# Loading the x0 steps of a CIN tower straight from their rows in DRAM, without the four-fold copy

## What is computed

```python
def cin(embeddings, W0, W1, W2):
    x0 = xk = embeddings                       # (1024, 32, 16)
    outs = []
    for W in (W0, W1, W2):                     # W0 (32, 32, 64), W1 and W2 (32, 64, 64)
        xk = relu(einsum('bmd,bhd,mhk->bkd', x0, xk, W))
        outs.append(sum(xk, axis=2))
    return concatenate(outs, axis=1)           # (1024, 192)

e = stack([tbl_f[ids[:, f]] for f in range(32)], axis=1)
h = concatenate([cin(e, W0, W1, W2), dense_ctx], axis=1)
h = maximum(h @ W_top1 + b_top1, 0)
h = maximum(h @ W_top2 + b_top2, 0)
y = h @ W_top3
```

## Time and profile before

| | before |
|---|---|
| device time, median of 3 runs | 718.49 us |
| lowest and highest | 717.80 and 718.72 us |
| span of the profiled execution | 715.9 us |
| DVE busy | 600.3 us, 84% |
| PE busy | 599.1 us, 84% |
| POOL busy | 524.6 us, 73% |
| SP's DMA queue | 178.22 MB, 66.0% of 16 engines' time |
| `x0_copies` written from `x0_rows` | 28 DMAs, 12 MB |
| loads from `x0_copies` | 83 DMAs |

### The profile page before, as it was taken

How to read it: one execution, slowest core, us unless ns; L and a number is a source line. 1 busy time by engine, 2 the same in 40 slices (tenths; PEclk the granted TensorE clock), 3 DMA queues, 4 the chain that set the end, 5 groups by cost and what they waited for, 6 DMA issues and landing times.

```text
span 715.9 us, 8322 instructions
## 1 busy us (share of the span) xinstructions
PE 599.1 (84%) x2592; PEld 192.4 (27%) x2592; DVE 600.3 (84%) x442; ACT 237.5 (33%) x388; POOL 524.6 (73%) x383
## 2 busy tenths in 40 slices
PE   2057859898987998898698988897979999999998
PEld 1053213232322222222222222232322232223333
DVE  0004997899999999999969999999999999999750
ACT  1004251615233241616124251616152526151413
POOL 6777778778888888787587888688887385738530
PEclk9569988999999999999899999999999999999999
DMA  4239899596949877595919877596939696927000
GB/s 102 65 89 393 311 352 388 199 381 244 369 152 329 347 271 293 187 402 216 396 43 334 340 270 295 184 400 223 399 125 358 245 390 240 393 87 278 0 1 0
DMA packets 64662, 180.58 MB, mean 252 GB/s; under 512 B 10033, under 2 KB 22193, under 8 KB 64642
## 3 DMA queue, kind: packets, MB, share of 16 engines
q1 hardware_dynamic: 56450, 178.22, 66.0%
q0 software_dynamic: 8192, 2.11, 2.6%
HBM read 176.63 MB, written 16.26 MB: 269 GB/s over the span
## 4 chain that ended last, share of the span: by engine, by line
POOL 34%; issue 20%; PE 15%; DVE 15%; DMA 8%; ACT 6%; SPq 1%; DVEq 0%; POOLq 0%; ACTq 0%
POOL gathered L482 18%; POOL pool_ring L521 12%; PE acc L797 11%; DVE dve_ring L667 10%; DMA x_wide<-x_copies 8%; POOL pool_ring L482 4%; ACT x_ps L572 3%; ACT x_sb L582 2%; PE x_ps L823 2%; DVE z_half L682 2%; DVE l_tiles L704 2%; DVE features L689 1%; ACT layer_out L576 1%; SPq L358 0%; DMA idx<-in_ids 0%
## 5 line engine op out<-in xcount | busy, mean ns | idle before, releaser
L667 DVE TENSOR_TENSOR dve_ring<-x_wide,x_ps 128x1024 f32<-128x1024 f32 (+1 forms) x328 | 446.4, 1423 | 30.6 <-ACT x_ps L572 26.1
L797 PE MATMUL acc<-dve_ring,w_sb 128*64 128x512 f32 x1576 | 380.7, 607 | 40.4 <-DVE dve_ring L667 38.5
L521 POOL TENSOR_TENSOR pool_ring<-x_wide,x_sb 128x1024 f32<-128x1024 f32 x118 | 280.0, 2379 | 79.8 <-ACT x_sb L582 46.8
L482 POOL DMA_INDIRECT gathered<-in_tbl,idx x224 | 213.5, 953 | 72.9 <-issue 64.8
L797 PEld LDWEIGHTS acc<-dve_ring,w_sb 128*64 128x64 f32 x1576 | 106.3, 139 | 297.9 <-issue 147.3
L797 PE MATMUL acc<-pool_ring,w_sb 128*64 128x512 f32 x472 | 127.0, 618 | 29.1 <-POOL pool_ring L521 29.1
L572 ACT ACTIVATE x_ps<-acc 64x512 f32<-64x512 f32 x128 | 73.0, 570 | 134.3 <-PE acc L797 125.0
L576 ACT ACTIVATE layer_out<-acc 128x512 f32<-128x512 f32 x48 | 28.7, 597 | 165.0 <-PE acc L797 164.2
L582 ACT COPY x_sb<-layer_out 64x512 f32<-64x512 f32 x128 | 79.0, 617 | 3.4
L704 DVE TENSOR_TENSOR l_tiles<-x_wide,x_rot_ps 128x1024 f32<-128x1024 f32 x32 | 38.5, 1209 | 47.8 <-DMA x_wide<-x_copies 47.8
L769 PE MATMUL acc<-l_tiles,w_sb 128*64 128x512 f32 x256 | 61.2, 599 | 4.0 <-DVE l_tiles L704 3.5
(11 more groups left out here) (36 smaller groups left out, 100.4 us busy)
## 6 DMA issues: line engine op xcount, KB each, us to landing
x_wide<-x_copies SPq DMA_DIRECT2D x58, 2048.0 KB, 11.7
l_tiles<-x_copies SPq DMA_DIRECT2D x16, 1024.0 KB
x_copies<-x_rows SPq DMA_DIRECT2D x14, 768.0 KB
x_wide<-x_copies SPq DMA_DIRECT2D x6, 1536.0 KB, 13.4
x_rot<-x_rows SPq DMA_DIRECT2D x64, 128.0 KB, 4.2
gathered<-in_tbl,idx POOLq DMA_INDIRECT x224, 2.4
x_wide<-x_copies SPq DMA_DIRECT2D x3, 1024.0 KB, 9.0
x_rows<-x_t SPq DMA_DIRECT2D x7, 256.0 KB, 6.7
```

What stands on the lines that cost most here:

```text
L482: pool.indirect_dma_start(into[:, f * DIM:(f + 1) * DIM], None, tables[f], bass.IndirectOffsetOnAxis(ap=idx[:, slot, f:f + 1], axis=0)).th ...
L521: nc.gpsimd.tensor_tensor(pool_ring[:, slot, :], x0_step(h, layer, t), x_sb[layer - 1][:], ALU.mult).then_inc(pool_made, 1)
L667: nc.vector.tensor_tensor(dve_ring[:, slot:slot + width, :], x0_step(h, layer, t, width).rearrange("p (s n) -> p s n", n=WIDE), x_ps[layer ...
L797: last = nc.tensor.matmul(acc[h][c * HK:(c + 1) * HK, :], w_sb[layer - 1][:, step_at(layer, t), :], tile[:, c * CHUNK:(c + 1) * CHUNK], st ...
```

## The change

`x0_copies`, its writes and its two semaphores are gone. `load_steps` now takes its rows from `x0_rows`, and issues one DMA for each step of 128 partitions: 512 KB, whose source runs over 32 rows, each named four times by a dimension of stride 0, with 4 KB for each name. A block is four such DMAs, a load of layer 0's operands two, and the waits on their semaphores count accordingly. `load_operands` waits for the staging of the tile where it waited for the copies. At the start the parts are staged without a wait after each, and one wait stands before the loads.

```diff
-            def copy_rows(tile, h, first, last):
-                src = rows_of(tile)[first:last, h * WIDE:(h + 1) * WIDE].unsqueeze(1).broadcast_to([last - first, Q, WIDE])
-                dst = x0_copies[bass.ts(2 * tile + h, COPIED * Q), :].rearrange("(f q) n -> f q n", q=Q)
-                sp.dma_start(dst[first - FIRST_FIELD:last - FIRST_FIELD], src).then_inc(x0_copied[h], 16)
...
             def load_steps(dst, tile, h, first, apart, sem):
-                rows = x0_copies[bass.ts(2 * tile + h, COPIED * Q), :][first * Q:]
+                rows = rows_of(tile)[FIRST_FIELD + first:, h * WIDE:(h + 1) * WIDE]
                 row = rows.ap[0][0]
-                src = bass.AP(rows.tensor, rows.offset,
-                              [[row, P], [apart * Q * row, dst.ap[1][1]], list(rows.ap[1])])
-                sp.dma_start(dst, src).then_inc(sem, 16)
+                for i in range(dst.shape[1]):
+                    src = bass.AP(rows.tensor, rows.offset + i * apart * row, [[row, FIELDS], [0, Q], [1, WIDE]])
+                    sp.dma_start(dst[:, i, :], src).then_inc(sem, 16)
...
             def load_operands(tile, h, p):
-                sp.wait_ge(x0_copied[h], copied(tile))
+                sp.wait_ge(x0_staged, staged(tile))
...
                     stage(0, place, (j, j + 1))
                     parts += 1
-                sp.wait_ge(x0_staged, 16 * parts)
-                for h in range(2):
-                    for field, place in fields:
-                        copy_rows(0, h, max(field, FIRST_FIELD), min(field + F_TILE, FIRST_FIELD + COPIED))
+            sp.wait_ge(x0_staged, 16 * parts)
             load_rot(0, 0)
-            sp.wait_ge(x0_copied[0], copied(0))
             load_near(0, 0)
...
-                    if start:
-                        copy_tile(1, 1)
-                    if h == 1 and there(it, 2):
-                        copy_tile(it + 2, 0)
-                        copy_tile(it + 2, 1)
...
-                eng.wait_ge(near_loaded[p], 16)
+                eng.wait_ge(near_loaded[p], 32)
...
         def block_loads(it, h, block):
-            return 16 * (it + 1) if block < 2 else 16 * (2 * it + h + 1)
+            if block >= 2:
+                return 16 * BLOCK * (2 * it + h + 1)
+            if isinstance(it, int) and 2 * it + h < NEAR_FIRST:
+                return 16 * (BLOCK - 1)
+            return 16 * BLOCK * (it + 1) - (32 if h == 0 else 16)
...
-                        dve.wait_ge(far_loaded, 16 * (p + 1))
+                        dve.wait_ge(far_loaded, 32 * (p + 1))
```

More of the change, by code:

```diff
@@ L41 @@
 FIRST_FIELD = 4
-COPIED = FIELDS + STEPS
 ROW_TILES = ROWS // P
@@ L154, in cin_tower @@
         x0_rows = nc.dram_tensor("x0_rows", (TILES * KEPT, DIM * P), F32, kind="Internal").ap()
-        x0_copies = nc.dram_tensor("x0_copies", (TILES * 2 * COPIED * Q, WIDE), F32, kind="Internal").ap()
         x0_wide = sb("x0_wide", [P, 6, BLOCK * WIDE])
@@ L222, in cin_tower @@
         rot_loaded = sem("rot_loaded")
-        x0_copied = [sem(f"x0_copied{h}") for h in range(2)]
         near_loaded = [sem(f"near_loaded{p}") for p in range(NEAR_FIRST)]
@@ L274, in block_loads @@
         def block_loads(it, h, block):
-            return 16 * (it + 1) if block < 2 else 16 * (2 * it + h + 1)
+            if block >= 2:
[3 more added lines that the diff above has]
+            return 16 * BLOCK * (it + 1) - (32 if h == 0 else 16)
         def staged(tile):
             return 16 * (KEPT // F_TILE) + 32 * tile
-        def copied(tile):
-            return 16 * (KEPT // F_TILE + tile)
         def rows_of(tile):
@@ L334, in stage_tile @@
                 stage(tile, ROW_TILES, (0, KEPT // F_TILE - ROW_TILES))
-            def copy_tile(tile, h):
-                if h == 0:
-                    sp.wait_ge(x0_staged, staged(tile))
-                    sp.nop(nofuse=True)
-                copy_rows(tile, h, FIRST_FIELD, FIRST_FIELD + COPIED)
             def load_steps(dst, tile, h, first, apart, sem):
-                rows = x0_copies[bass.ts(2 * tile + h, COPIED * Q), :][first * Q:]
+                rows = rows_of(tile)[FIRST_FIELD + first:, h * WIDE:(h + 1) * WIDE]
                 row = rows.ap[0][0]
-                src = bass.AP(rows.tensor, rows.offset,
-                              [[row, P], [apart * Q * row, dst.ap[1][1]], list(rows.ap[1])])
-                sp.dma_start(dst, src).then_inc(sem, 16)
+                for i in range(dst.shape[1]):
+                    src = bass.AP(rows.tensor, rows.offset + i * apart * row, [[row, FIELDS], [0, Q], [1, WIDE]])
+                    sp.dma_start(dst[:, i, :], src).then_inc(sem, 16)
             def load_block(tile, h, blk):
@@ L421, in _ @@
             load_block(0, 0, 3)
-            sp.wait_ge(x0_copied[1], copied(0))
             load_near(0, 1)
@@ L441, in body @@
                             load_block(it + h, 1 - h, blk)
-                        if start and blk == 2:
-                            copy_tile(1, 0)
                         if blk == 2 and h == 1 and there(it, 2):
```

## The result

| | before | after |
|---|---|---|
| device time, median | 718.14 us | 724.65 us |
| lowest and highest, 4 runs each | 717.73 and 718.72 us | 723.21 and 727.82 us |
| span of the profiled execution | 715.9 us | 721.8 us |
| DVE busy | 600.3 us | 595.1 us |
| SP's queue | 178.22 MB, 66.0% | 165.64 MB, 64.7% |

The ratio is 1.0095, with a 95% interval of 1.007 to 1.012: slower, by some 6.5 us, which is under 1% but clear of the interval. The time lies within the range that was forecast, but the likeliest case, 719.0, did not come true.

What follows compares the result with a forecast made beforehand. POOL's gathers set the pace until about 103 us, then DVE. All terms were 0 except 0.5 us of late issues: span 715.9 + 0.5 = 716.4, plus 2.6 to the median, 719.0 us; range 712.5 to 727.

Steps and rivals of the forecast that it cites:

- its own signs: Signs against it: DVE waiting for blocks mid-program, batch rate 370 GB/s or less, POOL's products moving, pause at 345 gone.
- rival 1: Within batches each piece costs the DMA engines extra, making block 3 late: 722 at 0.12 us, 730.8 at 0.2; chance 0.16.
- What the copies were worth: Mid-program, removing 28 DMAs (30.6 us of DMA time) gains nothing, as no load stands behind them: term 0.
- The start: DVE starts 2 to 4 us earlier, 3 taken, hidden by PE's wait for POOL until 103.25 us: term 0.
- The issues: On SP's queue, 205 more issues, 0.65 us (0.55 to 1.1) each; uncovered only at 599.24, 0.47 us.
- The rate: Loads within a batch: reading a DRAM row four times costs nothing, 411 GB/s beside 405: term 0.
- rival 4: Pieces read through 32 rows, written to 128 partitions, move badly: some 845 at half rate, near 1100 strictly; chance 0.05.
- Rival 2: POOL's 6.13 us pause between two gathers from 345.03 goes with the change: -5.7 us, 713.3; chance 0.12.
- Rival 3: DVE's early start reaches the end of the program: -3 us, 716.0; chance 0.07.
- Rival 5: SP becomes late, 4.7 us of its time per block: batches with h = 0 exceed cover, +2 us, 721; chance 0.09.
- The cover: At block 3's products, lateness is covered for 1.4 us with h = 0, 0.8 with h = 1: term 0.
- The sum: Span 715.9 + 0.5 = 716.4 us, plus 2.6 from span to run median: 719.0; chance 0.48.

Runs made afterwards that it cites:

- run 1: Kernel before, copies kept, each load of steps cut into one 512 KB DMA per step (288 for 83): 717.87 us beside 717.66, ratio 1.0.
- the run of section 4: Changed kernel, but reading rows of an embedding table, 32 rows 4 KB apart, each named four times: 717.56 us, ratio 0.9991.
- the run at 16 KB: Changed kernel with rows of x0_rows 16 KB apart instead of 8, a tile staged in 7 DMAs instead of 2: 728.35 us, ratio 1.0156.

## Why the prediction was right, and where it was wrong

By its own signs the prediction was wrong in its mechanism: DVE has waits for blocks in the middle of the program, and the rate of the batch, 326 to 339 GB/s, is below the 370 that it named. That the time lies in the range is luck. The range reached to 727 for the sake of rival 1, a cost of each piece, which run 1 shows to be nothing; the loss has another cause, to which the prediction gave term 0. Of its terms:

**What the copies were worth: right.** Term 0 in the middle of the program; 717.58 us without them.

**The start: the direction right, the size wrong.** DVE's first product came at 56.23 us instead of 57.76, 1.5 us and not 3 earlier, and the next two starts lost more than that:

```profile
56.23 2.35 DVE L678 TENSOR_TENSOR l_tiles<-x_wide,x_rot_ps 128x1024 f32<-128x1024 f32 x2 [45.38 <-DMA x_wide<-x_rows]
62.99 2.35 DVE L678 TENSOR_TENSOR l_tiles<-l_tiles,x_rot_ps 128x1024 f32<-128x1024 f32 x2 [4.40 <-DMA l_tiles<-x_rows]
72.06 17.86 DVE L641 TENSOR_TENSOR dve_ring<-x_wide,x_ps 128x1024 f32<-128x1024 f32 x11 [6.71 <-ACT x_ps L546]
```

That POOL's pace covers this until 103 us held, on the losing side: its first product came at 103.44 instead of 103.25, and PE's wait for it shrank from 6.66 to 2.32 us, where a longer one was forecast:

```profile
105.87 1.08 PE L771 MATMUL acc<-pool_ring,w_sb 128*64 128x512 f32 x4 [2.32 <-POOL pool_ring L495]
```

**The issues: right, a little low.** Duration in ns, min/median/max, of the new form:

```profile
L334 SPq DMA_DIRECT2D x_wide<-x_rows x256: 534/577/3547, 49.6 to 654.0; - x128
```

With its address a piece takes 0.72 to 0.76 us of SP's time where 0.65 was forecast. Run 1, with as many pieces, and the run of section 4 with this very form at 4 KB, 717.56 us, show that it costs the program nothing.

**The rate: the step that failed.** It is the sentence "Reading a row of DRAM four times instead of four copies of it: the copies did that already, at 411 GB/s beside 405 of the loads. Term 0." The loads went from 405 to 339 GB/s, and this, with what follows from it, is the whole loss as far as these runs can tell: with the spacing mended the ratio is 1.0006 (0.9997 to 1.0016). Two things were wrong with it. It asked whether a row may be read four times, and didn't ask where the rows lie: `x0_copies` had its rows side by side, `x0_rows` has them 8 KB apart, since both halves share a row. And it took the rate of a stretch of 2.5 us, DRAM to DRAM, for that of loads into SBUF. That the copies read the very same rows at 411 GB/s is true, and why they weren't slowed is open. The destination, the order and the length of the stretch all differ. The same holds for the 406 GB/s beside which rival 4 was given 0.05: a stretch of 1 us in which other loads were under way.

One page bears on this. The Trainium skill, "DMA: Bandwidth & Descriptors", section "Latency and other measured facts", has a row on the row pitch in HBM at large powers of two: copies run at 207 GB/s at a pitch of 512 KiB and at 103 at 4 MiB, and 4 KiB of padding bring the full rate back. The runs here agree on the cure, 334 to 385 GB/s with 4 KB of padding, and show an effect already at 8 KB, of which the page says nothing, where rows of 4 KB are read. The page calls its mechanism, streams that meet in the same channel of the memory, an inference; here no run shows a mechanism either. At 512 KB of distance nothing was tried. The rule that the prediction weighed, from "Rules for kernel authors" on the same page of the Trainium skill, at least 1 MiB per DMA, is not borne out by run 1: 512 KB pieces that stand in a queue run at 396 GB/s, whole blocks at 397.

**The rivals.** Rival 1 gave the effect, late blocks and a slower program, but not the mechanism: pieces cost nothing of their own, bytes do. Rival 4 came nearest, with a source that moves badly, but it blamed the shape, 32 rows to 128 partitions, and that shape moves at 382 GB/s when the rows lie 4 KB apart; and it priced the rate at half, where it was five sixths. Had the working of rival 4 been done at 339 GB/s, 10.0 million bytes would take 29.5 us of a phase of 39, and the step from there to the end would have been the cover of a block, as in rival 1. Rival 2: the stall did not go but grew, to 7.89 us. Rival 3: nothing arrived. Rival 5: SP's lateness in run 1 cost nothing.

**The cover: the place was missed.** The prediction looked at block 3 and found 0.8 and 1.4 us. Block 3 is waited for once, 0.85 us at 280.22. Block 0, which comes behind it in the queue, is the one that DVE waits for eight times, because layer 0 waits for the whole of it. The row that hinted at waits of layer 0 was the 0.42 us at 599.24, for block 1, and I took it for a place of its own. That DVE's regular pauses take up lateness was right, and it is a part of why 17.7 us of waits became 5.9. That POOL's stall is longer where the loads are slower was not in the prediction at all.

**The sum.** The 2.6 us that it adds to the span are not the distance within one execution, which is 1.75 to 1.88 us in the executions on record (723.60 beside 721.8); the rest fits a profiled execution that was faster than the median.

## What to carry over

When a layout changes, compare not only bytes and descriptors but the distance between the rows that one DMA reads: a power of two above the length of a row is worth an experiment with a little padding, which here is one number. The busy share of the DMA engines doesn't show it (1.00 and 1.02); the GB/s beside it do. Take them at the same place of a batch in both kernels: between fixed times, 338 to 360 us, the run at 16 KB shows 284 GB/s at a share of 0.86, only because its batch begins 6.6 us later. And a rate is a term only for the same direction, shape and length of stretch as the row it was read from.

## What the runs showed of the hardware

- Rows of 4 KB, 32 to a DMA and read four times each, into SBUF, mean of five batches: 382 GB/s at a distance of 4 KB, 385 at 12, 326 and 334 at 8, 350 at 16. 128 different rows: 396 side by side, 353 at 8 KB.
- The four pieces of a block don't land evenly when the rate is low. In the batch of 255 us after, the third and the fourth piece of block 2, issued 0.7 us apart, took from issue to landing:

```profile
x_wide<-x_rows SPq DMA_DIRECT2D x1, 512.0 KB, 6.9
x_wide<-x_rows SPq DMA_DIRECT2D x1, 512.0 KB, 12.9
```

- POOL's stall before the 178th gather, of 6.1 to 8.7 us and longer where the loads are slower, and three stalls, 56 gathers apart, with 8 KB of memory for descriptors.
